# Two-layer transformer on one Trainium2 core: the causal mask of the first attention set by GpSimd on the scores in SBUF instead of by TensorE products

## The reference, cut to what matters

```python
dot = jnp.einsum('bhid,bhjd->bhij', q, k)
q_norm_sq = jnp.sum(q * q, axis=-1, keepdims=True)
k_norm_sq = jnp.sum(k * k, axis=-1, keepdims=True)
vals = q_norm_sq + k_norm_sq.transpose(0, 1, 3, 2)
scores = dot * dot / (vals - 2.0 * dot + EPSILON) * SCORE_SCALE
mask = jnp.triu(jnp.ones((Lq, Lq), dtype=scores.dtype), k=1) * -1000000000.0
scores = scores + mask[None, None, :, :]
attn = jax.nn.softmax(scores, axis=-1)
out = jnp.einsum('bhij,bhjd->bhid', attn, v)
```

## Time and profile before

| | us |
|---|---|
| median of 3 runs (lowest to highest) | 3171.81 (3169.41 to 3182.85) |
| the profiled execution: device time | 3176.6 |
| its span in the trace | 3174.6 |
| PE busy (28516 instructions) | 2825.4, 89% |
| DVE busy (6131) | 2363.9, 74% |
| ACT busy (3686) | 2039.8, 64% |
| POOL busy (3054) | 1747.2, 55% |

### The profile page before, as it was taken

One profiled execution on the slowest core, in us unless ns is written; L12 is line 12 of the kernel. 1 busy time (PEld: TensorE's weight loads), 2 busy tenths in 40 slices (PEclk: granted clock), 3 DMA queues, 4 the chain that ended last, 5 costly groups with the idle time before them and its releaser, 6 DMA issues. The chain is left out here.

```text
span 3174.6 us, 76595 instructions
## 1 busy us (share of the span) xinstructions
PE 2825.4 (89%) x28516; PEld 1976.1 (62%) x28516; DVE 2363.9 (74%) x6131; ACT 2039.8 (64%) x3686; POOL 1747.2 (55%) x3054
## 2 busy tenths in 40 slices
PE   2899999999999999988997788888888888789998
PEld 1677677777667777642332566666666666556666
DVE  2899899998889989855233566766666666489998
ACT  1888888888888888842332355555555555467776
POOL 1666666666666666634110355555555655466665
PEclk8999999999999999987998799999999999999999
DMA  5333333333333333310000645443544444000001
GB/s 159 64 64 64 64 63 64 63 61 59 57 57 61 63 59 64 64 40 5 1 0 1 112 70 89 71 86 70 84 77 77 79 76 87 7 8 21 27 21 34
DMA packets 109266, 181.96 MB, mean 57 GB/s; under 512 B 26336, under 2 KB 95712, under 8 KB 96416
## 3 DMA queue, kind: packets, MB, share of 16 engines
q1 hardware_dynamic: 105440, 176.28, 30.5%
q10 hardware_dynamic: 3456, 0.79, 0.2%
HBM read 115.92 MB, written 60.29 MB: 56 GB/s over the span
## 5 line engine op out<-in xcount | busy, mean ns | idle before, releaser
L789 POOL TENSOR_TENSOR ratio_scores<-ratio_scores,ratio_max_cols 128x512 f32<-128x512 f32 (+3 forms) x1024 | 725.7, 724 | 374.0 <-DVE ratio_max_cols L699 369.9
L1273 DVE TENSOR_REDUCE zeroed_max_cols<-bank 128x1 f32<-128x512 f32 (+3 forms) x1024 | 445.7, 480 | 192.4 <-PE bank L185 190.8
L182 PE MATMUL bank<-ratio_k_stack,ratio_q_stack 102*128 102x512 bf16 (+7 forms) x2048 | 510.9, 305 | 81.8 <-DMA ratio_k_stack<-ratio_norms_k 46.7
L1166 ACT ACTIVATE zeroed_prob<-bank 128x512 f32<-128x512 f32 x640 | 376.8, 593 | 300.3 <-PE bank L1056 206.2
L699 DVE CUSTOM_DVE_ANT_0 ratio_scores<-bank,ratio_scores 128x512 f32<-128x512 f32 (+3 forms) x1024 | 472.4, 489 | 22.1
L689 DVE TENSOR_TENSOR ratio_scores<-bank,ratio_inverse 128x512 f32<-128x512 f32 x640 | 436.3, 682 | 57.0 <-PE bank L182 42.3
L561 ACT ACTIVATE ratio_prob<-bank 128x512 f32<-128x512 f32 x640 | 378.3, 592 | 124.0 <-PE bank L475 123.0
L472 PE MATMUL bank<-const_f_sb,ratio_scores 128*128 128x128 f32 x2560 | 413.0, 275 | 3.0 <-ACT ratio_prob L561 2.5
L550 ACT ACTIVATE ratio_inverse<-bank 128x512 f32<-128x512 f32 x640 | 381.7, 597 | 51.2 <-PE bank L185 50.9
L1385 POOL TENSOR_SCALAR_AFFINE_SELECT zeroed_prob<-zeroed_prob 128x256 f32<-128x256 f32 (+1 forms) x640 | 228.1, 365 | 333.2 <-ACT zeroed_prob L1166 331.5
L185 PE MATMUL bank<-const_b_sb 128*128 128x128 bf16 x2048 | 391.9, 223 | 1.7 <-issue 1.7
(11 more groups left out here) (169 smaller groups left out, 5612.0 us busy)
## 6 DMA issues: line engine op xcount, KB each, us to landing
ratio_q_stack<-ratio_parts_q SPq DMA_DIRECT2D x192, 128.0 KB
ratio_k_stack<-ratio_parts_k SPq DMA_DIRECT2D x192, 128.0 KB
zeroed_q_stack<-zeroed_parts_q SPq DMA_DIRECT2D x192, 128.0 KB, 4.4
zeroed_k_stack<-zeroed_parts_k SPq DMA_DIRECT2D x192, 128.0 KB, 7.6
ratio_parts_q<-ratio_parts SPq DMA_DIRECT2D x96, 128.0 KB
ratio_parts_k<-ratio_parts SPq DMA_DIRECT2D x96, 128.0 KB
zeroed_parts_q<-zeroed_parts SPq DMA_DIRECT2D x96, 128.0 KB
zeroed_parts_k<-zeroed_parts SPq DMA_DIRECT2D x96, 128.0 KB
```

The costliest lines, as they stand in the source:

```text
L182: i = e.matmul(bank[:, off:off + w], qs[0:rows, s, hh, ib * P:(ib + 1) * P], ks[0:rows, s, hh, 0:w], start=(k == 0), stop=mask is None, sk ...
L789: i = e.tensor_tensor(seg, seg, mx[:, pair % M_BUFS, c:c + 1].to_broadcast([P, w]), ALU.subtract)
L1166: e.activation(prob[:, n % FOLD_PROBS, 0:wd], exp_banks[n % 2][:, 0:wd], ACT.Exp, scale=0.25).then_inc(s["prob"])
L1273: i = e.tensor_reduce(mx[:, pair % FOLDS, c:c + 1], bank[:, off:off + (ib + 1) * P], AX_X, ALU.max)
```

## The change

The mask product disappears from `turn`, which now has four transposes per unit and nothing else. POOL gets a new step `mask(n)`: one affine select that writes -1e9 into the diagonal blocks of `scores`, in place, above the diagonal (128 columns for a unit with one diagonal block, 256 for one with two). It stands one unit behind `less`: after `less(n)` comes `mask(n - 1)`, and ahead of the preparation step and the bias step. `turn(n)` waits for the new semaphore `masked` in place of `lessened`. The mask matrix for the scores leaves the constants. The row maxima are taken before the mask, as they were.

```diff
-B_IDENT, B_DENOM, B_SCORE, B_MAX1 = 0, 128, 256, 384
-B_COLS = 512
+B_IDENT, B_DENOM, B_MAX1 = 0, 128, 256
+B_COLS = 384
...
-    b[:, B_SCORE:B_SCORE + P] = MASK_SCORE * (row > col)
...
             def turn(n):
                 bank = exp_banks[n % 2]
-                q.wait_ge(s["lessened"], n + 1)
+                q.wait_ge(s["masked"], n + 1)
                 q.wait_ge(s["prob"], n - 1)
-                first = True
-                for _, ib, off in UNITS[n % N_UNITS]:
-                    wd = (ib + 1) * P
-                    for jb in range(ib + 1):
-                        at = slice(off + jb * P, off + (jb + 1) * P)
-                        e.matmul(bank[:, at], scores[:, n % S_BUFS, at], net.ident,
-                                 is_transpose=True, start=first, stop=False, skip_group_check=True)
-                        first = False
-                    i = e.matmul(bank[:, off + wd - P:off + wd], net.ident_b, net.mask(B_SCORE),
-                                 start=False, stop=True, skip_group_check=True)
+                for t in range(T):
+                    at = slice(t * P, (t + 1) * P)
+                    i = e.transpose(bank[:, at], scores[:, n % S_BUFS, at], net.ident)
                 i.then_inc(s["turned"])
...
+            def mask(n):
+
+                blocks = [off // P + ib for _, ib, off in UNITS[n % N_UNITS]]
+                to = scores[:, n % S_BUFS, :].rearrange("p (k t) -> p k t", k=T)
+                diagonal = to[:, blocks[0]:T:max(blocks[-1] - blocks[0], 1), :]
+                q.wait_ge(s["lessened"], n + 1)
+                e.affine_select(diagonal, diagonal, [[0, 2]][:len(blocks) - 1] + [[-1, P]], ALU.is_ge, dropped, 0, 1).then_inc(s["masked"])
...
+            dropped = e.to_reg(MASK_SCORE)
...
                 if n < total:
                     less(n)
+                if 0 < n <= total:
+                    mask(n - 1)
                 step = ratio_prep_at(n, halves)
```

More of the change, by code:

```diff
@@ L273 @@
     norm_hi norm_mid norm_lo parts_q parts_k norms_q norms_k gathered0 gathered1 q_ones k_ones v_ones
-    denoms log_den inverse dots weighed maxima lessened post_filled post_read
+    denoms log_den inverse dots weighed maxima lessened masked post_filled post_read
     turned prob attended o_group rec_den x_bias"""
```

## The result

The changed kernel takes 3195.69 us (median of 10 runs, 3177.10 to 3206.53); the kernel before takes 3176.57 us in its 10 runs (3169.41 to 3185.25). The ratio is 1.0057, with a 95% interval of 1.0037 to 1.0077: 18 us slower, 12 to 24. The forecast was 4 us slower, 3176, with a range of 3153 to 3197. The sign was right and the size was not: the result is inside the range by 1.3 us, but outside the band of 16 us around 3176 that was given 0.55.

What follows compares the result with a forecast made beforehand. No single engine bounds it, but a chain of 81.00 us a row, PE's part 8%. Terms -4.4 - 0.5 + 6.1 + 3.2 = +4.4 us on the 3171.8 median gave 3176, range 3153 to 3197.

Steps and rivals of the forecast that it cites:

- rival C: In the dense stretch POOL becomes the bound and `turn` waits for `masked`: 1 to 2 us a row, 3188 to 3204; chance 0.11.
- POOL's k step: Selects ahead of POOL's k-side preparation (L776) delay it by 0.38 us in each row's second half: +6.1 us over 16 rows.
- The products: Removing 1024 mask products from PE saves only those on the chain, 4.4 us, and 0.5 us in the tail.
- POOL's time: 640 selects add 234 us to POOL in the first attention, 871 to 1105 of 1301 us, still under the other engines.
- The new wait: `turn` waiting for `masked` costs nothing: three units of DVE's work, 4.6 us, cover POOL's lag, some 1 us to spare.
- VectorE's casts: DVE's casts and scaling meeting POOL's work in a row's first half, dealt anew: -0.3 us a row, bounds -1.6 and +1.3.
- the gather that caps: In a row's first half the last gather is nearly late, capping DVE's gain near 0.2 us a row; +0.2 taken, 3.2 us.
- A: PE is the path after all, so half of its 56 us comes through: 3144 to 3150, or 3155; chance 0.17.
- B: The port lock deals badly: selects block two more casts or scalings and the gather is late, +21 us, 3193; chance 0.17.
- D: PE's granted clock falls to 1.2 GHz in one row of twenty: 5 us, inside the forecast, sharing its 0.55.

Runs made afterwards that it cites:

- r4_bn_before: The kernel before, with VectorE's scaling of rows 1 to 15 replaced by statistics of the same length: 0.9984 of before, median 3173.4 us.
- r3_bn_after: The changed kernel, with VectorE's scaling of rows 1 to 15 replaced by statistics of the same length: 1.0008 of before, median 3183.8 us.
- r10_defer: The changed kernel, with the selects of units 3 to 5 of each half held back past POOL's preparation step for the k side: 1.0045 of before.
- r2_nomask: The changed kernel with the select left out altogether, so the first attention's scores are unmasked and `turn` waits for `lessened`: 0.9995 of before.
- r6_bias_after: The changed kernel, with POOL's four bias steps of a row moved from the next row's first half to units 31, 33, 35 and 37: 1.0011 of before.

## Why the prediction was right in its sign and short in its size

The forecast named more than a time. The select's two durations came as stated, and so did the k step's delay in the second half (0.3 us). The period was to be 81.0 to 81.6 us and is 83.4 in the mean (81.85 before), POOL was to be 85% busy and is 81%, and PE's waits for the gather in mid-row were to stay under 0.5 us and reach 1.59, the first row left out. That the range holds the result is luck in part: its upper end was drawn out towards rival C, whose cost did not come. The kernel before, measured again, was itself 4.8 us above the 3171.81 of the forecast, which took the result from 3190 to the edge. The sign is not luck, since the largest term, POOL's k step, is a cost that the experiments confirm.

**The products, -4.9 us.** Measured with the select left out: -1.6 us, -6 to +3. The step stands within its interval, and so does its main point: with three engines near 90%, 56 us of PE's time is worth hardly anything. That the chain passes over PE for only 8% of a row agrees with it.

**POOL's time, covered as a whole.** The durations are right (0.43 and 0.29 us, 239 us in all). That the work is "covered" is where the prediction was thin. As a share of the stretch it is. It even had POOL fall behind by 2 to 3 us in the dense stretch, but asked only what these arrears do to `turn`, not what they do to VectorE.

**The new wait, at nothing.** Right: 6.3 us in 17 pieces on the loads' side and 0.3 us on the matmuls'.

**POOL's k step, +6.1 us.** The prediction took +0.38 us in the second half and +0.72, hidden, in the first. Measured are +0.28 and +0.52, and the first is hidden indeed (37.96 against 37.95 us with the scaling gone). The price in the second half is larger than the delay itself in the single profiled executions (+0.8 us from k to q between `r4_bn_before` and `r3_bn_after`, +1.0 between before and after, 1.1 regained by `r10_defer`, each uncertain by some 0.4). Over all ten executions it is 0.6, 10 us in all. The 8 us between `r3_bn_after` and `r4_bn_before` are this term less the saved products; with the 1.6 us of `r2_nomask` it is some 10, against 6.1 forecast, and 6.1 is within what is uncertain in it.

**VectorE's casts, and the gather that caps: +3.2 us.** This is the step that failed. I dealt the three meetings of the first half anew as -0.4, -0.8 and +0.9. The cast of the norms gained as said (1.26 to 0.52 us). The k cast found no gap and lost 0.36 (0.90 to 1.26). The scaling lost not 0.9 but 2.1 us (1.03 to 3.12, each in the row shown). The rule that I worked with, that a held instruction comes in at the end of POOL's current one, was read from casts with an idle POOL behind them. It does not hold for the scaling where POOL is in arrears. The scaling's part alone measures 10 us, uncertain by 9 (the 18 of the change less the 8 that remain without the scaling), where the whole term had 3.2; by the rows it is 0.44 us a first half (38.40 less 37.96), 7 us. The cap of +0.2 us a row on this term rested on a gather that is nearly late, and in `r10_defer` the scaling costs its 0.87 us without one.

**The Trainium skill's rule** on the shared ports (SBUF — State Buffer, "SBUF: two separate sides") speaks of an exclusive lock for a whole instruction. That accounts for a hold of one instruction. The 2.80 us of the first scaling in this trace span six instructions of POOL, so the measurement goes beyond it.

**The rivals.** A is refuted by `r2_nomask`. B (the lock deals badly) is what happened, at its lower end and with its price on one instruction instead of three. C fails in its wait: POOL fills the dense stretch, yet `turn` waits for it only 6.3 us in all. POOL's arrears are there, and the long holds fall on them. For D, the clock is 0.98 against 0.99, and `r2_nomask`, which has the same 0.98, is no slower.

## What to carry to other kernels

Ask of a helper engine not only whether its share stays under the others', but where it falls behind, and which instruction of another engine has to get through there. A load that fits in the mean can put it in arrears just where a neighbour's instruction needs its turn. Here moving other work out of that stretch regained nominally 15 of the 18 us, and with the order around the k step put right the kernel became faster than before. And before crediting a saving on a busy engine, follow one period of the chain and count what stands on it.

## What the runs showed of the hardware

A scaling on VectorE from SBUF to SBUF (0.41 us alone) can be held by GpSimd over many of GpSimd's instructions, not just one: up to 3.75 us for a single instruction in the changed kernel, against 0.92 before:

```profile
L640 DVE TENSOR_SCALAR ratio_xn<-x,mean_var,rstd x64: 398/413/3750, 33.4 to 1280.4; 128x256 f32<-128x256 f32 x64
```

At other times it comes in at the end of GpSimd's running instruction and lengthens the next, as in `r6_bias_after` (1.33 us in place of 1.18 for two subtractions), or as the k cast does with the select of 0.59 us. The long holds all fall where GpSimd is two or more subtractions in arrears; what decides between the two cases stays open. Statistics (0.416 us), and VectorE's operations that read PSUM and one tile in SBUF (the maxima, the product with the reciprocals), kept their durations beside the fullest POOL.
